# A Flamingo block with gated attention and a mixture of experts: the row maximum written negated and used as the exponential's bias

## What is computed

```python
scores = jnp.einsum('bhnrd,bhncd->bhnrc', qb, kc)
scores = jnp.where(valid[None, None], scores.astype(jnp.float32), neg_inf)
attn = jax.nn.softmax(scores, axis=-1).astype(q.dtype)
out = jnp.einsum('bhnrc,bhncd->bhnrd', attn, vc)
...
x = x + jnp.tanh(g_xattn[0]) * _L0_xattn_ref(...)
x = x + jnp.tanh(g_ffn[0]) * _L0_ffn_ref(_layernorm(x, axis=-1), ...)
```

## Time and profile before

| What | Value |
|---|---|
| median of 3 runs | 553.26 us (552.57 to 554.41) |
| span of the profiled execution, first to last instruction | 547.9 us |
| median less span: launch, end and the difference between executions | 5.4 us |
| TensorE busy over the span | 474.1 us, 87% |
| VectorE busy over the span | 378.4 us, 69% |
| mean granted TensorE clock | 0.957 of full speed |

### The profile page before, as it was taken

The page is one execution under the profiler, slowest core; times in us unless marked ns, Lnnn a source line. Parts: engine busy times, 40 slices in busy tenths (PEclk is TensorE's granted clock), DMA queues, the critical chain, the costliest instruction groups (busy, mean ns, idle before and its releaser), DMA issues. The chain is left out here.

```text
span 547.9 us, 10716 instructions
## 1 busy us (share of the span) xinstructions
PE 474.1 (87%) x3469; PEld 436.0 (80%) x3469; DVE 378.4 (69%) x942; ACT 299.3 (55%) x756; POOL 210.1 (38%) x271
## 2 busy tenths in 40 slices
PE   5599998899989776219979999999999999999990
PEld 4388887677767664219979999998999989999990
DVE  6878989999998998736758584484853757644340
ACT  3689778687778763316546463373732736424130
POOL 8536768687868556420120303202132021221121
PEclk9899999999999998559999999999999999999996
DMA  8858331314132511164626463255551554111011
GB/s 272 203 129 211 67 75 46 77 41 78 49 70 67 195 51 52 38 215 144 214 40 211 97 214 93 25 140 162 142 166 19 136 173 136 18 18 16 11 19 19
DMA packets 41137, 56.80 MB, mean 104 GB/s; under 512 B 3721, under 2 KB 38064, under 8 KB 39040
## 3 DMA queue, kind: packets, MB, share of 16 engines
q1 hardware_dynamic: 34656, 48.10, 30.2%
q0 software_dynamic: 6144, 8.07, 8.7%
q10 hardware_dynamic: 288, 0.00, 0.0%
HBM read 36.24 MB, written 16.19 MB: 96 GB/s over the span
## 5 line engine op out<-in xcount | busy, mean ns | idle before, releaser
L544 POOL DMA_INDIRECT out_tokens<-ysc,rows x32 | 50.6, 1581 | 252.8 <-DVE ysc L1142 181.0
L1431 PE MATMUL bank<-bXh,wh 128*128 128x384 f32 (+1 forms) x384 | 123.1, 321 | 7.8 <-PEq L1506 3.0
L1432 PE MATMUL bank<-bXl,wh 128*128 128x384 f32 (+1 forms) x384 | 122.3, 319 | 0.0
L1433 PE MATMUL bank<-bXh,wl 128*128 128x384 f32 (+1 forms) x384 | 122.3, 318 | 0.0
L752 ACT ACTIVATE sil<-bank 128x384 f32<-128x384 f32 (+1 forms) x96 | 43.8, 456 | 112.8 <-PE bank L1433 112.8
L1128 DVE TENSOR_TENSOR hF<-sil,bank 128x384 f32<-128x384 f32 (+1 forms) x96 | 48.9, 510 | 79.7 <-ACT sil L752 79.7
L635 ACT ACTIVATE p<-bank,nb 128x128 f32<-128x128 f32 x256 | 73.5, 382 | 32.0 <-DVE nb L927 31.9
L1431 PEld LDWEIGHTS bank<-bXh,wh 128*128 128x128 f32 x384 | 73.2, 190 | 9.1 <-issue 6.3
L1431 PE MATMUL bank<-wh,hH 128*128 128x256 f32 x256 | 73.1, 286 | 0.3 <-DVE ysc L1142 0.3
L1432 PEld LDWEIGHTS bank<-bXl,wh 128*128 128x128 f32 x384 | 73.1, 190 | 0.0
L1433 PEld LDWEIGHTS bank<-bXh,wl 128*128 128x128 f32 x384 | 73.0, 190 | 0.0
(11 more groups left out here) (146 smaller groups left out, 867.4 us busy)
## 6 DMA issues: line engine op xcount, KB each, us to landing
stage<-in_w12T SPq DMA_DIRECT2D x16, 1024.0 KB, 4.8
stage<-in_w3T SPq DMA_DIRECT2D x8, 1024.0 KB, 5.7
expert_rows<-padrow SPq DMA_DIRECT2D x8, 662.5 KB, 8.0
rows<-expert_rows SPq DMA_DIRECT2D x7, 662.5 KB, 4.3
kM<-k SPq DMA_DIRECT2D x64, 64.0 KB, 2.4
cT<-in_ctxT SPq DMA_DIRECT2D x8, 256.0 KB, 3.4
out_tokens<-x_all SPq DMA_DIRECT2D x8, 256.0 KB, 2.3
x_all<-in_x SPq DMA_DIRECT2D x2, 640.0 KB, 8.3
```

What stands on the lines that cost most here:

```text
L544: pool.indirect_dma_start(out=out, out_offset=bass.IndirectOffsetOnAxis(rows[par][:, c, D + E:ROW].bitcast(U32), 0), in_=ysc[par][:, c, :] ...
L1431: nc.tensor.matmul(out_ap, ah, bh, start=start, stop=False)
L1432: nc.tensor.matmul(out_ap, ah, bl, start=False, stop=False)
L1433: return nc.tensor.matmul(out_ap, al, bh, start=False, stop=stop)
```

## The change

`exp_bias` and its semaphore go. The row reduction writes its result negated, and that is the bias of the exponential, so `p` is now at most 1. The factor 16384 moves behind the transposes: ScalarE's fp16 copy scales by it, and VectorE's instruction for the rest multiplies by it and subtracts in one, which makes a `scalar_tensor_tensor` of a `tensor_tensor`.

```diff
-PSCALE = 9.704060527839234
+PSCALE = 16384.0
...
             def exps(G, g, early):
-                act.wait_ge(dve_bias, G + 1)
+                act.wait_ge(dve_max, G + 1)
...
-                    ins = act.activation(p32[g % 2][:, h, :], S[g % 2][:, h * T:(h + 1) * T], ACT.Exp, bias=nb[g % 2][:, h:h + 1])
+                    ins = act.activation(p32[g % 2][:, h, :], S[g % 2][:, h * T:(h + 1) * T], ACT.Exp, bias=nm[g % 2][:, h:h + 1])
...
-                act.activation(pT[g % 2][:, 0, :, :], Tb[g % 2][:, :].rearrange("p (h t) -> p h t", h=GH), ACT.Copy).then_inc(act_hi, 1)
+                act.activation(pT[g % 2][:, 0, :, :], Tb[g % 2][:, :].rearrange("p (h t) -> p h t", h=GH), ACT.Copy, scale=PSCALE).then_inc(act_hi, 1)
...
             def largest(G, g):
                 dve.wait_ge(pe_s, G + 1)
-                dve.tensor_reduce(nm[g % 2][:, :], S[g % 2][:, :].rearrange("p (h t) -> p h t", t=T), AX_X, ALU.max)\
+                dve.tensor_reduce(nm[g % 2][:, :], S[g % 2][:, :].rearrange("p (h t) -> p h t", t=T), AX_X, ALU.max, negate=True)\
                    .then_inc(dve_max, 1)
-
-            def exp_bias(G, g):
-
-                dve.wait_ge(dve_max, G + 1)
-                dve.tensor_scalar(nb[g % 2][:, :], nm[g % 2][:, :], -1.0, PSCALE, ALU.mult, ALU.add).then_inc(dve_bias, 1)
...
-                dve.tensor_tensor(pT[g % 2][:, 1, :, :], Tb[g % 2][:, :].rearrange("p (h t) -> p h t", h=GH), pT[g % 2][:, 0, :, :],
-                                  ALU.subtract).then_inc(dve_lo, 1)
+                dve.scalar_tensor_tensor(pT[g % 2][:, 1, :, :], Tb[g % 2][:, :].rearrange("p (h t) -> p h t", h=GH), PSCALE,
+                                         pT[g % 2][:, 0, :, :], ALU.mult, ALU.subtract).then_inc(dve_lo, 1)
...
-                    if cur:
-                        exp_bias(G, g)
```

More of the change, by code:

```diff
@@ L96, in gated_block @@
         nm = [sb(pa, f"nm{i}", [P, GH], F32) for i in range(2)]
-        nb = [sb(pa, f"nb{i}", [P, GH], F32) for i in range(2)]
         p32 = [sb(pa, f"p32_{i}", [P, GH, T], F32) for i in range(2)]
@@ L203, in gated_block @@
         pe_v, pe_bo, dve_bo, act_vf, act_v1, pool_vr, act_v2, pool_v3 = (sem(n) for n in ("pe_v", "pe_bo", "dve_bo", "act_vf", "act_v1", "pool_vr", "act_v2", "pool_v3"))
-        pe_s, dve_max, dve_bias, act_exp = (sem(n) for n in ("pe_s", "dve_max", "dve_bias", "act_exp"))
+        pe_s, dve_max, act_exp = (sem(n) for n in ("pe_s", "dve_max", "act_exp"))
         pe_t, act_hi, dve_lo, pe_pv, dve_os, dve_rec, dve_on = (sem(n) for n in ("pe_t", "act_hi", "dve_lo", "pe_pv", "dve_os", "dve_rec", "dve_on"))
```

## The result

The changed kernel took 549.17 us (median of ten runs, 547.03 to 550.87), the kernel before 553.21 (ten runs on the same chip): medians 4.0 us apart. The ratio with its 95% interval, which is not the quotient of these two medians, is 0.9937 (0.9919 to 0.9956), or 3.5 us (2.4 to 4.5). Twelve more runs in a later timing gave 549.54 against 552.84 and a ratio of 0.9949 (0.9929 to 0.9969), or 2.8 us (1.7 to 3.9). So the gain is 3 to 4 us, and the timing alone can't tell it from the 2.9 us of the forecast. The forecast was 550.4 in 545.5 to 554.3.

The account below looks back on a forecast made before the run. It took VectorE, coupled to GpSimd in a loop of 24.80 us per body, to bound the attention. Body gains of -1.27, -0.30, -0.30 and -1.0 sum to -2.87 us: span 545.0, median 550.4, range 545.5 to 554.3.

Parts of the forecast that it names:

- the sum: All predicted gains by body: -1.27 (body 3), -0.30 (bodies 4 and 5), -0.30 (body 6), -1.0 (body 7), together -2.87 us.
- The two halves at no cost: Scaled fp16 copy and rest by `scalar_tensor_tensor`: taken at old prices, 0 added, upper bound 0.255 us for the rest.
- Small VectorE instructions stand still behind GpSimd's, and that is what the bias costs: Some small SBUF instructions on VectorE wait until a GpSimd instruction ends; `nb` takes 170 ns in the median, 3248 at most.
- Bodies 0 to 2 nothing: No gain there: TensorE nearly full in the first two, the third's gain given back in body 3.
- Given back in group 3, by `oN` standing where `nb` stood: The 0.68 us gained per body is lost in group 3, as `oN` stands through `V`, `xbo` and `k`.
- the 0.15 of the sum: Bodies 4 and 5 gain GpSimd's gap ahead of `k`, 0.15 us each.
- Body 3 1.27: `pT` of group 3 starts 0.85 us earlier, `prob` falls into `xn`, so `pT` of group 5 comes 1.27 earlier.
- Body 7 1.0: No `k` follows: `pT` behind `oN` starts 0.88 us earlier, group 7 adds 0.18; -1.06, rounded to -1.0.
- The 0.18 of group 7: Removing the bias instruction in group 7, where `nb` has its ordinary 0.17, gains 0.18 us with the wait's overhead.
- The same 5.4 us between span and median: The profiled span of 547.9 us lies 5.4 below the median; forecast span 545.0 became median 550.4.
- The rule against the row: Skill's first-to-issue port lock would let `oN` in at `V`'s end; trace agrees in body 2, not in 3, 4, 7.
- The first rival: In group 3 `oN` slips in between `V` and `xbo`: 546.5 us (544.5 to 548.9), chance 0.20.

Follow-up runs that it names:

- the kernel with the halves only: Kernel before with the factor 16384 moved to the fp16 copy and the rest, `nb` kept: 552.20 us, ratio 0.9987.
- the unused bias: Changed kernel with the old `tensor_scalar` put back on VectorE, writing a tile nobody reads: 552.73 us, ratio 0.9996.
- the bias by an instruction that does not stand still: Changed kernel with a separate `nb` written by a negating `tensor_reduce`, the exponentials waiting for it: 550.97 us, ratio 0.9954.
- the bias-only kernel: Changed kernel without the factor 16384 and with the old `tensor_tensor` for the rest: 549.27 us, ratio 0.9923.
- the seam kernel: Changed kernel with the last of GpSimd's four indirect DMAs of bodies 2 to 6 moved between the next body's `xbo` and `k`: 545.29 us, ratio 0.9856.
- the one with the keys first: Changed kernel with ScalarE writing the keys ahead of its copy of the high halves in group 3, from body 2 on: 549.55 us, ratio 0.992.
- two DMAs moved: Kernel before with the last two indirect DMAs of bodies 2 to 6 moved between the next body's `V` and `xbo`: 554.33 us, ratio 1.0002.

## Why the prediction was nearly right

The direction and the range held, and so did the half of the mechanism that says what the bias instruction costs. The other half, where VectorE stands once it is gone, held in body 7 only: the sign named for it, `oN` of 2.5 to 3 us to the end of `k` in bodies 3 to 5, did not come (1.88, 0.31 and 0.31 us). The gain was under-sized, 2.9 against 4.0 us in the medians and 4.6 at the attention's end, and there is luck in its being this near: bodies 0 to 6 gave 3.83 us for the 1.87 of the sum, and body 7 gave less than its part.

*The two halves at no cost*: right, 684 against 683 ns, and shown alone by the kernel with the halves only.

*Small VectorE instructions stand still behind GpSimd's, and that is what the bias costs*: right. With the unused bias the timing shows no gain; the bias by an instruction that does not stand still leaves about half or more.

*Bodies 0 to 2 nothing*: wrong by 0.93, of which 0.50 lies before group 3 of body 0. I took TensorE as full there and did not follow the instructions one by one. In body 0 `oN` asked at 35.13 and stood 1.27 us behind `q`; now it asks at 34.35 and takes 0.29.

*Given back in group 3, by `oN` standing where `nb` stood*: right in body 7 and in the bias-only kernel, but not in bodies 4 to 6 of the changed kernel itself, where `oN` passes behind `xbo` and the loss is `k` late by 0.61 instead. Both forms cost nearly the same: the period is 24.57 with the one and 24.44 with the other, and I had 24.65. So bodies 4 and 5 gained 0.38 and 0.37 for the 0.15 of the sum, body 6 0.43 for 0.30.

*Body 3 1.27*: it was 1.72, since `oN` was released at `xbo`'s end, not at `k`'s: from `V` to `pT` of group 3 it is 2.48 us and was 4.54 (93.70 to 98.24).

*Body 7 1.0*: it was 0.75 to the last `pT`. The step itself was right: from `V` to `pT` of group 3 it is 2.48 us and was 3.32, 0.84 less for the 0.88 worked out. The 0.18 of group 7 did not arrive. In the second profile of the changed kernel body 7 gives only 0.32, with the same 2.48 in its own group 3 (190.70 for `V`); why the rest is lost there is open.

*The same 5.4 us between span and median*: this was no launch cost. The timed runs show 1.8 us around the span (547.03 with a span of 545.2); the other 3.6 were the profiled execution's luck. As a constant on both sides of the difference it did no harm, but the span of a single profile would have misled by more than 1 us.

*The rule against the row.* The first rival, that `oN` gets in at the seam of `V` and `xbo`, was not borne out in body 7 or body 3. In the direction of the time it had something: that VectorE passes and `prob` asks in time is what the seam kernel does, for 545.3.

## What to carry to other kernels

Where a VectorE instruction of a few elements shows a long time, look what GpSimd does at its end, and look at the seam between two GpSimd instructions: VectorE always got in where the second was recorded 0.07 us or more behind the first's end, and mostly not where it was recorded 0.06 to 0.08 us ahead of it (16 of 68). Removing one such instruction hands the stall to the next candidate, so the change to look for is a gap in GpSimd's list at the place where VectorE asks, made of work that is there anyway. A wait's total in the list of waits says little of its worth: 15 us less for ScalarE brought 4, and TensorE's 3.9 us for `V` brought nothing.

## What the runs showed of the hardware

**Seams.** In the fourteen traces (those of this study, from 21 to 213 us) I took each `nb`, `oN`, `prob`, `lgs` and `lse` that was at least 0.15 us over its plain time and in progress as a GpSimd instruction (not a DMA) ended, and sorted by the recorded distance to GpSimd's next instruction. The starts and lengths of GpSimd's instructions are rough in these records, so the classes are those of the record and not of the engine. At 0.07 us or more the VectorE instruction ended there, within 0.35 us, in all of the 264 cases. At -0.02 it went on in both of 2 cases. At -0.03 to -0.05 it ended there in 77 and went on in 5. At -0.06 to -0.08 it ended there in 16 (12 of them ahead of a copy of two elements) and went on in 52, through one, two or three GpSimd instructions, for up to 3.53 us (the unused bias in body 3). That a gap lets `oN` in is shown at one place, by the kernel with the seam and the one without it; there a DMA instruction stands in the gap, but in body 3 of the changed kernel the gap ahead of `k` is empty (0.41 us), and `oN` got in too. Whether an overlap of 0.04 and one of 0.07 are different things is open. It is not only the kind of instruction: `nb` at the end of `V` with `xbo` behind it got in all 10 times at 0.04 to 0.05 (bodies 1 and 2) and went on all 15 times at 0.06 to 0.08 (bodies 3 to 7), and what else sets these bodies apart is not known.

The Trainium skill (SBUF — State Buffer, section "Who interferes with whom") has issue order decide who blocks whom. In this kernel's traces that is not enough: with two DMAs between `V` and `xbo`, `oN` asks at 120.58, `xbo` starts at 120.73, and `oN` waits for it and for `k`. The same section says that a `tensor_reduce` never contends on trn2, while `tensor_scalar` and a `tensor_tensor` with two SBUF inputs can; the 0.16 us of the reduction against the 1.94 of the same four elements by `tensor_scalar` agree.

**The clock.** Between executions of one kernel there are steps of about 2 us that have nothing to do with its code. The windows of 22 to 27 us, of the changed kernel and then of the one with the seam:

```profile
22.00:27.00 5.00, 4.32 (x20) 3.08 (x19) 5.00 (x21) 4.31 (x14) 2.40 (x3) 0.83 1.09 324
```

```profile
22.00:27.00 5.00, 4.17 (x13) 2.78 (x13) 4.63 (x21) 3.37 (x11) 2.66 (x3) 0.50 1.09 317
```

The granted clock is 0.50 there in the second, the lower level of 1.2 GHz throughout, and group 3 of body 0 comes 2.0 us later (29.97 for 27.96). Up to there the two programs are alike. Four of the fourteen traces have 0.50 in this window, and group 3 of body 0 starts in them at 29.77 to 30.30; in the other ten it is 0.80 or more, and 27.96 to 28.79. Two of the seam kernel's six runs took 547.12 (the profiled one) and 547.56, at a mean granted clock of 0.942 and 0.941, the other four 545.12 to 545.39 at 0.948; that the second of the slow pair had the same cause is likely, but it has no trace. A second place is the start of the experts, where TensorE stands for 3.0 us in both traces (to 277.15 and 273.32): from 274 to 282 us the clock is 1.00 in the profiled execution before and 0.86 in the one after.

**Left open.** In bodies 4 to 6 of the changed kernel (both profiles) and of the one with the keys first, VectorE's maximum of group 3 starts 1.2 to 1.4 us after the recorded end of the scores it waits for (scores to 116.53, maximum at 117.89), and in the changed kernel ScalarE's copy 1.0 us after the transposes (to 116.97, copy at 117.95); in the bias-only kernel both are 0.04 us, with the same order of instructions. The recorded ends are modelled. The late maximum starts within 0.15 us of the end of TensorE's matmuls for the router (L1218, to 117.76), which come after the scores. The lateness of `k` in the changed kernel seems to hang on it, and what causes it I did not find. When VectorE can pass while GpSimd runs a DMA instruction is open too: `nb` passes under one at 139.59 in the kernel before and doesn't at 120.61 with two DMAs moved.
